# A recurrence of 1024 steps: a filler matmul or a denser piece of attention in each step

## The chip, the cores and the metric

The kernel runs on one core of a Trainium2 chip. The metric is device time in microseconds of one execution. Three runs of the kernel before took 1089.88, 1085.83 and 1089.57 us; the median is 1089.57.

## The reference, cut to what matters

The model is a small image network: four blocks, each a token mixer and a feed-forward part, on x of shape (2, 32, 32, 32): two images, 1024 pixels each, 32 channels. The third block's feed-forward part (L2 in the kernel) is a recurrence over the 1024 pixels in order. From inputs W, V, gamma, beta it computes, in words:

```
x : (2, 1024, 32)            # after a layer norm
wx = batch_norm(x @ W.T)     # gamma, beta; statistics over all tokens
h_0 = 0
h_t = sigmoid(wx_t + h_(t-1) @ V.T)      # t = 1 .. 1024, for both images
x = x + h
```

The fourth block's mixer (L3) is attention in windows of 8x8 and 16x16 pixels and across windows. Its input is the residual stream with the states of that recurrence added:

```
sim = einsum('bnhid,bnhjd->bnhij', qh * SCALE, kh) + pos
attn = softmax(sim, axis=-1)
out = einsum('bnhij,bnhjd->bnhid', attn, vh)
```

Since a window covers pixels next to each other, its attention can start as soon as the recurrence has passed its last pixel.

## The kernel before, in words

The program is a sequence of blocks. `recurrent(tag, swept, use, beside)` is called for L0 (swept, with another algorithm: many segments advanced at once, three sweeps, lines 896 to 926) and for L2 (not swept: one step after another). This case is about the second call.

Its first block does the layer norm (`Norm.pe`, with 11 filler matmuls from `keep_streaming`, line 95, which multiply a constant tile of ones into a dead PSUM bank), the product with W (line 786), batch statistics and the scaled input, written into `yx`. Column pair t of `yx` holds, in its upper 32 rows, the input of step t for both images and, in its lower 32 rows, the state.

Its second block is the loop. Step t is one matmul of TensorE, `v` (64x32, V and the identity stacked) times two columns of `yx`, into PSUM (line 844), and one sigmoid of ScalarE from PSUM back into the next two columns (line 856). The matmul waits for the semaphore `state`, the sigmoid for `preact`. In fp32 a matmul is two weight loads and two matmul records in the trace.

`Front` holds the part of the L3 attention that is done within the loop. `front.pe` and `front.pe_bulk` are Python generators that issue TensorE's instructions for it piece by piece: each `yield` ends a piece. From step HALF + 5 = 517 on, the loop calls `next(others)` once after each step, so that at most one piece stands between two steps; `for _ in range(n): yield` is n steps without a piece, in which VectorE does the work that the next piece waits for. The first half's pixels are taken at step 512, three eighths more at 896 (`BULK`), the last 128 after the loop. The pieces are: products of the query and key weights (line 1676), transposes of x (1509) and of the normed x (1519), projections (1592), values and across-window products (1694, 1700, 1705), scores (1447, 1449), transposes of the scores (1610). TensorE's queue is in program order, so a piece stands ahead of the next step's matmul.

VectorE's side (`dve`, `dve_bulk`) is the layer norm of a part, copies out of PSUM, the biased scores (1457) and their shift by the least (1470), each behind semaphores. `rest` is the block after the loop, with the remaining attention.

Of the kernel before, what the change touches and what calls it, by code (L numbers as in the profile page):

```python
# [15 lines left out]
NB, SIDE, C = 2, 32, 32  # L16
# [722 lines left out]
def more(nc, io, loc):  # L739
    ctx, sig, sb, ps, chain, unchain, Norm = (loc[k] for k in ("ctx", "sig", "sb", "ps", "chain", "unchain", "Norm"))  # L740
    keep_streaming = loc["keep_streaming"]
# [6 lines left out]
    def recurrent(tag, swept, use, beside):  # L748
# [5 lines left out]
        with ExitStack() as st:  # L754
# [8 lines left out]
            with ExitStack() as s2:  # L763
# [6 lines left out]
                with nc.Block() as block:  # L770
# [8 lines left out]
                    def _(pe):  # L779
# [51 lines left out]
            with ExitStack() as s2:  # L831
                p_z = ps(tag + "p_z", [128, 2, BANK], stack=s2)
                if not swept:

                    HALF, BULK = T // 2, T - 128
                    front = beside(s2, by_batch)
                    with nc.Block() as block:
                        @block.tensor
                        def _(pe):
                            others = front.pe(pe)  # L840
                            for t in range(T):
                                if t:
                                    pe.wait_ge(s("state"), t)
                                pe.matmul(p_z[0:C, t % 2, 0:NB], v[:, 0:C], yx[:, NB * t:NB * (t + 1)], start=True, stop=True).then_inc(s("preact"), 1)  # L844
                                if t == BULK + 5:
                                    others = itertools.chain(others, front.pe_bulk(pe))
                                if t > HALF + 4:
                                    next(others, None)
                            for _ in others:
                                pass  # L850

                        @block.scalar
                        def _(act):
                            for t in range(T):
                                act.wait_ge(s("preact"), t + 1)
                                act.activation(yx[0:C, NB * (t + 1):NB * (t + 2)], p_z[0:C, t % 2, 0:NB], ACT.Sigmoid).then_inc(s("state"), 1)  # L856
# [495 lines left out]
    with ExitStack() as st:  # L1352
# [97 lines left out]

        def biased(dve, banks, u):
# [20 lines left out]
        def shifts_until(u):  # L1472
            return u + 1 - sum(1 for a in BY_ACT if a <= u)

        class Front:
# [28 lines left out]
            def turn(self, pe, part):  # L1504

                a, b = self.PARTS[part]
                pe.wait_ge(sig["part_added"], 3 * part + 3)
                for t in range(a, b):
                    ins = pe.transpose(self.p_tok[:, t * R:(t + 1) * R], x[:, t * 128:(t + 1) * 128], ident[0:R, 0:R])
                    if t == b - 1:  # L1510
                        ins.then_inc(sig["part_turned"], 1)
                    yield

            def turn_back(self, pe, part):

                a, b = self.PARTS[part]
                pe.wait_ge(sig["part_scaled"], part + 1)
                for t in range(a, b):
                    ins = pe.transpose(self.p_back[:, t % 4 * 128:(t % 4 + 1) * 128], xn_two[:, t - a], ident[:])
# [69 lines left out]
            def project(self, pe, part, g, dst):  # L1589
                a, b = self.PARTS[part]  # L1590
                for r, n, src in strips(g, xo[:, WITHIN[g]], 4 * a, 4 * (b - a)):
                    last = pe.matmul(dst[:, r * SIDE:(r + n) * SIDE], aqk[:, WITHIN[g]], src, start=True, stop=True)
                last.then_inc(sig["qk_made"], 1)
# [8 lines left out]
            def turn_scores(self, pe, u):  # L1602

                pe.wait_ge(sig["at_shifted"], u + 1)
                for n in range(2):
                    s = 2 * u + n
                    if s >= 2:
                        pe.wait_ge(sig["weights_in"], s - 1)
                    for j in range(NJ):
                        last = pe.transpose(self.turn_banks[n][:, j * 128:(j + 1) * 128], scored[:, u, j, n * 128:(n + 1) * 128], ident[:])  # L1610
                        if j == NJ - 1:
                            last.then_inc(sig["scores_turned"], 1)
                        yield
# [6 lines left out]
            def score_early(self, pe, u):  # L1620
                for n in range(1 if units[u][0] == 2 else 2):
                    for j in range(NJ):
                        ins = score(pe, self.early_banks[j], u, j, n)
                        if units[u][0] == 2 or n == 1:
                            ins.then_inc(sig["at_scores"], 1)
                    yield

            def value_pieces(self, pe, part, p_v):

                for slot, g, tiles in ((0, 2, (4 + part, 6 + part)), (1, 0, (4 + 2 * part, 5 + 2 * part))):  # L1630
                    for n, t in enumerate(tiles):
                        last = pe.matmul(p_v[:, (2 * slot + n) * JC:(2 * slot + n + 1) * JC], value_tokens(g, t), av[:, slot], start=True, stop=True)
                        if (slot, n) == (1, 1):
                            last.then_inc(sig["e_made"], 1)
                        yield

            def across_pieces(self, pe, part, p_3, p_1):

                cols = 3 * HEADS * HC
                for n in range(4):  # L1640
                    for b in range(NB):
                        last = pe.matmul(p_1[b * 64:(b + 1) * 64, n * cols:(n + 1) * cols], window1(8 + 4 * part + n), ae1[:, b], start=True, stop=True)
                    yield
                cols = NB * 3 * HEADS * HC
                for n in range(2):
                    last = pe.matmul(p_3[:, n * cols:(n + 1) * cols], window3(part, 2 + n), ae3[:], start=True, stop=True)
                    if n == 1:
                        last.then_inc(sig["e_made"], 1)
                    yield
# [21 lines left out]
            def pe(self, pe):  # L1671

                p_q, p_e = self.p_q, self.p_e
                pe.wait_ge(sig["load_at"], 16 * 14)
                for k in range(2):
                    last = pe.matmul(p_q[:, 0, k * 128:(k + 1) * 128], aq[:, k], ak[:, k], start=True, stop=True)
                    if k == 1:
                        last.then_inc(sig["qk_made"], 1)
                    yield
                yield from self.turn(pe, 0)  # L1680
                for _ in range(24):
                    yield
                yield from self.turn_back(pe, 0)
                for _ in range(6):
                    yield
                pe.wait_ge(sig["qk_read"], 1)
                for k, g in enumerate((2, 0)):
                    pe.wait_ge(sig["xo_made"], k + 1)
                    self.project(pe, 0, g, p_q[:, k])
# [713 lines left out]
```

## Time and profile before

| | |
|---|---|
| median of three runs | 1089.57 us |
| the profiled execution | 1091.56 us |
| its span, first to last instruction | 1089.6 us |
| TensorE busy | 726.1 us, 67% |
| ScalarE, VectorE, GpSimd busy | 447.6, 436.1, 255.3 us |
| mean granted clock of TensorE | 0.676 |
| matmuls of line 844 | 269.2 us busy, 2048 records |

The profile is of one execution. In it, PE is TensorE's matmuls and PEld its weight loads (they overlap), DVE is VectorE, ACT ScalarE, POOL GpSimd. PEclk is the share of TensorE's full clock (2.4 GHz) that was granted; it has two levels, 1.0 and 0.5, and a value between them is a mean over a stretch with both. Idle time of an engine stands with what ended it, behind an arrow.

### The profile page before, as it was taken

To read this page: it belongs to the slowest core of one execution; us is meant where nothing else is said; L and a number is where in the kernel's file an instruction comes from. 1 tells how busy PE (TensorE), PEld (TensorE's weight loads), DVE (VectorE), ACT (ScalarE), POOL (GpSimd) and SP (SyncE) were. 2 spreads that over 40 slices of the span, in tenths; PEclk is the share of its full clock that TensorE was granted. 3 is DMA by queue.
4 is the path that set the end of the run, shared out by engine and by line. 5 is a ranking of instruction groups with operands and counts; after the bars stand their busy time and mean duration, and the time that the engine had idled before them with its cause. 6 is when DMAs were issued, how large, how long until landed. Compare 5 with 4: busy or idle time off the path is not lost. (4 is left out here: it accounts for less than half of the span.)

```text
span 1089.6 us, 11684 instructions
## 1 busy us (share of the span) xinstructions
PE 726.1 (67%) x4350; PEld 414.4 (38%) x4361; DVE 436.1 (40%) x733; ACT 447.6 (41%) x1480; POOL 255.3 (23%) x153
## 2 busy tenths in 40 slices
PE   7907878888886787555555555558786555675776
PEld 4302333333343444233333333336554333453443
DVE  4697999999856554400000000021242000210653
ACT  4446767676635542333333333332222333223541
POOL 3378988898900000200000000000000000000310
PEclk9957999999995595655555555555555555555796
DMA  3020000000000000200000000000000000000000
GB/s 68 2 58 0 1 0 1 0 1 0 1 3 3 1 22 10 74 1 1 1 0 1 1 1 1 1 0 1 1 1 1 1 0 1 1 1 1 2 23 10
DMA packets 10017, 7.92 MB, mean 7 GB/s; under 512 B 7378, under 2 KB 8514, under 8 KB 9672
## 3 DMA queue, kind: packets, MB, share of 16 engines
q1 hardware_dynamic: 9960, 7.18, 2.7%
q8 instruction: 34, 0.56, 0.2%
q14 instruction: 23, 0.19, 0.1%
HBM read 5.34 MB, written 0.26 MB: 5 GB/s over the span
## 5 line engine op out<-in xcount | busy, mean ns | idle before, releaser
L844 PE MATMUL L2p_z<-L2yx,L2v 64*32 64x2 f32 x2048 | 269.2, 199 | 231.1 <-ACT L2yx L856 226.1
L856 ACT ACTIVATE L2yx<-L2p_z 32x2 f32<-32x2 f32 x1024 | 165.0, 161 | 383.5 <-PE L2p_z L844 383.5
L844 PEld LDWEIGHTS L2p_z<-L2yx,L2v 64*32 64x32 f32 x2048 | 181.4, 136 | 334.2 <-ACT L2yx L856 317.2
L630 POOL TENSOR_TENSOR hc<-hs,cb 128x1024 f32<-128x1024 f32 x64 | 149.4, 2355 | 20.9 <-DVE hs L613 20.9
L1499 DVE COPY xn<-L2yx 32x512 f32<-32x512 f32 (+1 forms) x2 | 0.8, 384 | 366.4 <-ACT L2yx L856 366.4
L1499 POOL COPY xn<-L2yx 32x128 f32<-32x128 f32 x1 | 0.3, 283 | 544.4 <-SPq L1827 544.4
L557 PE MATMUL p_y<-hc,ident 128*128 128x512 f32 x256 | 122.4, 600 | 5.0 <-DVE y_seq L596 2.8
L613 DVE TENSOR_TENSOR_SCAN hs<-d_a,p_bb 128x1024 f32<-128x1024 f32 x48 | 109.8, 2287 | 7.2 <-ACT d_a L580 1.1
L584 ACT ACTIVATE cb<-p_cb 128x1024 f32<-128x1024 f32 x64 | 65.0, 1016 | 6.0 <-PE p_cb L547 5.7
L557 PEld LDWEIGHTS p_y<-hc,ident 128*128 128x128 f32 x256 | 47.7, 191 | 49.9 <-issue 31.3
L580 ACT ACTIVATE d_a<-step,decay 128x1016 f32<-128x1016 f32 x48 | 54.6, 1138 | 24.1 <-DVE hs L613 23.5
L602 DVE TENSOR_TENSOR p_bb<-drive,p_bb 128x1024 f32<-128x1024 f32 x48 | 58.0, 1208 | 6.3 <-PE p_bb L541 6.3
L547 PE MATMUL p_cb<-c_parts,pick 96*128 96x512 bf16 x128 | 39.6, 391 | 11.9 <-ACT d_bu L589 10.5
L541 PE MATMUL p_bb<-b_parts,pick 96*128 96x512 bf16 x96 | 29.6, 391 | 20.4 <-DVE hs L613 19.4
L625 POOL TENSOR_TENSOR d_bu<-drive,d_bu 128x1024 f32<-128x1024 f32 x16 | 37.9, 2369 | 5.1 <-ACT d_bu L589 5.1
L906 PE MATMUL L0p_z<-L0yx,L0v 64*32 64x64 f32 x192 | 30.3, 305 | 9.9 <-PEq L770 4.4
L613 DVE TENSOR_TENSOR_SCAN hs<-p_bb,d_bu 128x1024 f32<-128x1024 f32 x16 | 36.2, 2264 | 0.0
L541 PEld LDWEIGHTS p_bb<-b_parts,pick 96*128 96x128 bf16 x96 | 8.3, 99 | 46.5 <-DVE hs L613 31.0
L906 PEld LDWEIGHTS L0p_z<-L0yx,L0v 64*32 64x32 f32 x192 | 17.5, 140 | 22.3 <-ACT L0yx L926 16.2
L926 ACT ACTIVATE L0yx<-L0p_z 32x64 f32<-32x64 f32 x96 | 20.1, 214 | 13.3 <-PE L0p_z L906 12.9
L547 PEld LDWEIGHTS p_cb<-c_parts,pick 96*128 96x128 bf16 x128 | 11.1, 98 | 37.9 <-ACT d_bu L589 18.8
L589 ACT ACTIVATE d_bu<-p_cb 128x1024 f32<-128x1024 f32 x16 | 16.4, 1024 | 18.1 <-PE p_cb L564 18.1
(485 smaller groups left out, 916.0 us busy)
## 6 DMA issues: line engine op xcount, KB each, us to landing
y_seq<-in_pick SPq DMA_DIRECT2D x1, 768.0 KB
b_parts<-part SPq DMA_DIRECT2D x3, 256.0 KB, 3.7
c_parts<-part SPq DMA_DIRECT2D x3, 256.0 KB, 4.4
pos<-in_pos SPq DMA_DIRECT2D x1, 512.0 KB, 3.6
ao<-in_at_o SPq DMA_DIRECT2D x1, 512.0 KB, 4.1
L1w<-in_L_w SPq DMA_DIRECT2D x1, 297.0 KB
L3w<-in_L_w SPq DMA_DIRECT2D x1, 297.0 KB
x_tok<-in_x SPq DMA_DIRECT2D x2, 128.0 KB, 3.0
```

What stands on the lines that cost most here:

```text
L541: last = pe.matmul(p_bb[:, u % 2, h * BANK:(h + 1) * BANK], pick[:, n], b_parts[:, k, c], start=True, stop=True)
L547: last = pe.matmul(p_cb[:, h * BANK:(h + 1) * BANK], pick[:, n], c_parts[:, k, c], start=True, stop=True)
L557: last = pe.matmul(p_y[:, c], ident[:], hc[:, v % RING, c], start=(n == 0), stop=(n == NS - 1))
L580: act.activation(dst[:, :, 1:L], src[:, :, 1:L], ACT.Exp, scale=decay[:, k, n:n + 1]).then_inc(sig["d_a"], 1)
L584: act.activation(cb[:, u % RING], p_cb[:], ACT.Copy).then_inc(sig["p_cb_read"], 1)
L602: dve.tensor_tensor(p_bb[:, u % 2], drive[:, k, c0:c0 + UC], p_bb[:, u % 2], ALU.mult).then_inc(sig["d_bu"], 1)
L613: dve.tensor_tensor_scan(hs[:, u % RING], decays, inputs, 0.0, ALU.mult, ALU.add).then_inc(sig["scanned"], 1)
L625: pool.tensor_tensor(d_bu_of(u), drive[:, k, c0:c0 + UC], d_bu_of(u), ALU.mult).then_inc(sig["d_bu_pool"], 1)
L630: pool.tensor_tensor(hc[:, u % RING], hs[:, u % RING], cb[:, u % RING], ALU.mult).then_inc(sig["hc"], 1)
L844: pe.matmul(p_z[0:C, t % 2, 0:NB], v[:, 0:C], yx[:, NB * t:NB * (t + 1)], start=True, stop=True).then_inc(s("preact"), 1)
L856: act.activation(yx[0:C, NB * (t + 1):NB * (t + 2)], p_z[0:C, t % 2, 0:NB], ACT.Sigmoid).then_inc(s("state"), 1)
L906: pe.matmul(p_z[0:C, f, 0:NB * n], v[:, 0:C], by_batch[:, cols], start=True, stop=True).then_inc(s("preact"), 1)
```

## The change

Each step of the L2 loop now carries either one filler, a bf16 matmul of 128x128 weights and 512 columns into a dead bank (`fill(FILL)`), or one piece of attention. Which of them is decided when the program is built: `beats` is a list of (nanoseconds, columns) of the steps so far, with 473 ns and 520 columns assumed for a filler step; each `yield` of a generator now says ahead of a piece how many nanoseconds and columns its step is to have (0, 0 for a rest); and `goes` lets the piece in only if the columns of the latest steps that fill 3413 ns, the piece's own among them, come to 3290 or more. Else the step takes a filler and the piece waits for the next.

The pieces themselves are made larger or smaller to fit: two or three transposes instead of one, four matmuls of the across-window products instead of one or two, projections cut into matmuls of 128 columns, the 256 keys of a score into two halves (`score_half`). The rests are recounted. Waits on semaphores move behind the yield. Step 0 is followed by five fillers. Ahead of the loop, 11 fillers follow the product with W, and 4 more the semaphore `shift`, which VectorE raises before it writes the scaled input. Both halves of the step's PSUM output now lie in bank 0 (`p_step`), since the filler writes bank 1. The L0 recurrence is not changed.

```diff
@@ recurrent, first block
                         if swept:
                             beside.pe_sum(pe, p_a)
                             beside.pe_square_sum(pe, p_a)
+                        else:
+                            keep_streaming(pe, p_a[:, 0:BANK], 11)
+                            pe.wait_ge(*at("shift", 1))
+                            keep_streaming(pe, p_a[:, 0:BANK], 4)
@@ recurrent, the loop
+                    FILL, STEP, WINDOW, LEAST = 512, 473, 3413, 3290
+                    p_step = p_z[0:C, 0].rearrange("p (n b) -> p n b", b=NB)
...
+                            def fill(columns):
+                                parts = (columns + BANK - 1) // BANK
+                                each = columns // parts // 16 * 16
+                                for _ in range(parts):
+                                    pe.matmul(p_z[:, 1, 0:each], stream[:, 0:128], stream[:, 0:each], start=True, stop=True)
+
+                            beats = [(STEP, FILL + 8)] * 8
+
+                            def goes(ns, columns):
+                                room, work = WINDOW - ns, columns + 8
+                                for length, did in reversed(beats):
+                                    part = min(length, room)
+                                    work += did * part / length
+                                    room -= part
+                                    if room <= 0:
+                                        break
+                                return work >= LEAST
+
                             others = front.pe(pe)
+                            ns, columns = next(others)
                             for t in range(T):
                                 if t:
                                     pe.wait_ge(s("state"), t)
-                                pe.matmul(p_z[0:C, t % 2, 0:NB], v[:, 0:C], yx[:, NB * t:NB * (t + 1)], start=True, stop=True).then_inc(s("preact"), 1)
+                                pe.matmul(p_step[:, t % 2], v[:, 0:C], yx[:, NB * t:NB * (t + 1)], start=True, stop=True).then_inc(s("preact"), 1)
+                                if t == 0:
+                                    fill(5 * BANK)
+                                    continue
                                 if t == BULK + 5:
+                                    assert not columns
                                     others = itertools.chain(others, front.pe_bulk(pe))
-                                if t > HALF + 4:
-                                    next(others, None)
-                            for _ in others:
-                                pass
+                                    ns, columns = next(others, (0, 0))
+                                if t > HALF + 4 and columns and goes(ns, columns):
+                                    beats.append((ns, columns + 8))
+                                    ns, columns = next(others, (0, 0))
+                                    continue
+                                if t > HALF + 4 and not columns:
+                                    ns, columns = next(others, (0, 0))
+                                beats.append((STEP, FILL + 8))
+                                if t < T - 1:
+                                    fill(FILL)
@@ Front.turn_scores, as an example of a generator
-                pe.wait_ge(sig["at_shifted"], u + 1)
                 for n in range(2):
                     s = 2 * u + n
-                    if s >= 2:
-                        pe.wait_ge(sig["weights_in"], s - 1)
                     for j in range(NJ):
+                        if j % 2 == 0:
+                            yield 600, 4 * 128
+                        if (n, j) == (0, 0):
+                            pe.wait_ge(sig["at_shifted"], u + 1)
+                        if j == 0 and s >= 2:
+                            pe.wait_ge(sig["weights_in"], s - 1)
                         last = pe.transpose(self.turn_banks[n][:, j * 128:(j + 1) * 128], scored[:, u, j, n * 128:(n + 1) * 128], ident[:])
                         if j == NJ - 1:
                             last.then_inc(sig["scores_turned"], 1)
-                        yield
@@ Front.pe, one of the recounted rests
                 yield from self.turn(pe, 0)
-                for _ in range(24):
-                    yield
+                yield from rests(28)
                 yield from self.turn_back(pe, 0)
```

What stands in TensorE's queue where the loop begins: `L2p_z<-L2yx,L2v` is the step, `stream` the filler, `L2p_w` the product with W. Before:

```order
L127 MATMUL L2p_b<-ident,xn_tok 64x128 x8
L786 MATMUL L2p_w<-xn,L2w 32x512 x4
L770 UNCONDITIONAL_BRANCH
L838 UNCONDITIONAL_BRANCH
L844 MATMUL L2p_z<-L2yx,L2v 32x2 x518
```

And after the change:

```order
L127 MATMUL L2p_b<-ident,xn_tok 64x128 x8
L786 MATMUL L2p_w<-xn,L2w 32x512 x4
L95 MATMUL L2p_a<-stream 128x512 x15
L770 UNCONDITIONAL_BRANCH
L844 UNCONDITIONAL_BRANCH
L869 MATMUL L2p_z<-L2yx,L2v 32x2
L850 MATMUL L2p_z<-stream 128x512 x5
L869 MATMUL L2p_z<-L2yx,L2v 32x2
L850 MATMUL L2p_z<-stream 128x512
```

Where 518 steps stood next to each other, each is now followed by a filler, and 15 fillers stand ahead of the loop (11 before the wait for `shift` and 4 behind it).

In TensorE's queue where a unit's scores are transposed (`scored` into the banks `atp_tok` and `atp_back`; `q` and `xo` are the scores' operands). Before:

```order
L1447 MATMUL atp_q<-xo,q 128x256 x2
L1447 MATMUL atp_e<-xo,q 128x256 x2
L844 MATMUL L2p_z<-L2yx,L2v 32x2 x3
L1610 MATMUL atp_tok<-ident,scored 128x128
L844 MATMUL L2p_z<-L2yx,L2v 32x2
L1610 MATMUL atp_tok<-ident,scored 128x128
L844 MATMUL L2p_z<-L2yx,L2v 32x2
L1610 MATMUL atp_tok<-ident,scored 128x128
```

And after the change:

```order
L869 MATMUL L2p_z<-L2yx,L2v 32x2
L1673 MATMUL atp_tok<-ident,scored 128x128 x2
L869 MATMUL L2p_z<-L2yx,L2v 32x2
L1673 MATMUL atp_tok<-ident,scored 128x128 x2
L869 MATMUL L2p_z<-L2yx,L2v 32x2
L1673 MATMUL atp_back<-ident,scored 128x128 x2
L869 MATMUL L2p_z<-L2yx,L2v 32x2
L850 MATMUL L2p_z<-stream 128x512
L869 MATMUL L2p_z<-L2yx,L2v 32x2
L850 MATMUL L2p_z<-stream 128x512
```

The transposes go in pairs, three pairs in a row and then fillers; a unit's eight transposes take four steps with a piece instead of eight. In the whole loop 945 steps carry a filler, 78 a piece, and the last neither.

## Rows read from the trace of the kernel before

**Rows 1.** The page, the span in 40 slices: busy shares and clock in tenths.
```profile
PE   7907878888886787555555555558786555675776
...
PEclk9957999999995595655555555555555555555796
```

**Rows 2.** The page's costliest groups: count, busy us, mean ns, idle before and releaser.
```profile
L844 PE MATMUL L2p_z<-L2yx,L2v 64*32 64x2 f32 x2048 | 269.2, 199 | 231.1 <-ACT L2yx L856 226.1
L856 ACT ACTIVATE L2yx<-L2p_z 32x2 f32<-32x2 f32 x1024 | 165.0, 161 | 383.5 <-PE L2p_z L844 383.5
```

**Rows 3.** Timeline, the loop's first two steps and last: start us, length us, engine.
```profile
454.58 0.23 PE L844 MATMUL L2p_z<-L2yx,L2v 64*32 64x2 f32 x2 [5.00 <-PEq L770]
...
456.05 0.26 PE L844 MATMUL L2p_z<-L2yx,L2v 64*32 64x2 f32 x2 [1.24 <-ACT L2yx L856]
...
1004.15 0.16 ACT L856 ACTIVATE L2yx<-L2p_z 32x2 f32<-32x2 f32 x1 [0.35 <-PE L2p_z L844]
```

**Rows 4.** A window: length; busy us of PE, PEld, DVE, ACT, POOL; granted clock; DMA.
```profile
750.00:775.00 25.00, 21.90 (x146) 18.46 (x146) 1.33 (x6) 6.65 (x42) 0.00 (x0) 0.50 0.00 1
```

**Rows 5.** Timeline, one step of the loop, and the 24th after it.
```profile
470.42 0.18 PEld L844 LDWEIGHTS L2p_z<-L2yx,L2v 64*32 64x32 f32 x2 [0.34 <-ACT L2yx L856]
470.42 0.26 PE L844 MATMUL L2p_z<-L2yx,L2v 64*32 64x2 f32 x2 [0.25 <-ACT L2yx L856]
470.72 0.16 ACT L856 ACTIVATE L2yx<-L2p_z 32x2 f32<-32x2 f32 x1 [0.35 <-PE L2p_z L844]
...
482.74 0.18 PEld L844 LDWEIGHTS L2p_z<-L2yx,L2v 64*32 64x32 f32 x2 [0.34 <-ACT L2yx L856]
```

**Rows 6.** Timeline, two matmul pairs of one shape, at full and at half clock.
```profile
330.65 0.27 PE L997 MATMUL L0p_a<-sm,ones 64*64 64x1 f32 x2
...
332.06 0.37 PE L1001 MATMUL L0p_a<-sm,ones 64*64 64x1 f32 x2 [1.13 <-DVE sm L1009]
```

**Rows 7.** Timeline, fillers of line 95: ten at full clock, five at half.
```profile
1057.21 2.32 PE L95 MATMUL L3p_b<-stream 128*128 128x512 bf16 x10 [0.16 <-issue]
...
426.11 2.34 PE L95 MATMUL e2p_b<-stream 128*128 128x512 bf16 x5 [0.33 <-issue]
```

**Rows 8.** Timeline, steps with a piece: a 128x128 product; a 16-column one.
```profile
721.84 0.18 PEld L844 LDWEIGHTS L2p_z<-L2yx,L2v 64*32 64x32 f32 x2 [0.23 <-issue]
...
722.76 0.18 PEld L844 LDWEIGHTS L2p_z<-L2yx,L2v 64*32 64x32 f32 x2 [0.23 <-issue]
...
752.35 0.61 PE L1694 MATMUL atp_e<-av,xo 128*128 128x16 f32 x2
...
752.88 0.18 PEld L844 LDWEIGHTS L2p_z<-L2yx,L2v 64*32 64x32 f32 x2
```

**Rows 9.** Timeline of the last matmuls ahead of the loop, and windows there.
```profile
448.51 1.06 PE L786 MATMUL L2p_w<-xn,L2w 32*32 32x512 f32 x8 [0.76 <-ACT xn L173]
...
450.00:452.00 2.00, 0.00 (x0) 0.00 (x0) 1.54 (x5) 0.29 (x1) 0.00 (x0) 0.85 1.06 369
```

**Rows 10.** Timeline of VectorE, its first work after the norm of the first part.
```profile
739.64 1.35 DVE L1549 COPY xo<-atp_back 128x512 f32<-128x512 f32 x3 [10.01 <-PE atp_back L1519]
```

**Rows 11.** Timeline behind the loop, TensorE's first product.
```profile
1004.62 1.19 PE L1566 MATMUL atp_tok<-L2yx,centre 32*128 32x128 f32 x4 [0.51 <-PEq L837]
```

**Rows 12.** Windows, columns as in rows 4.
```profile
350.00:355.00 5.00, 4.31 (x29) 2.53 (x28) 4.58 (x24) 2.90 (x15) 0.00 (x0) 0.50 0.00 0
440.00:442.00 2.00, 2.00 (x8) 0.84 (x7) 1.97 (x2) 0.00 (x0) 0.00 (x0) 0.71 0.00 0
1060.00:1065.00 5.00, 3.07 (x17) 1.27 (x18) 0.42 (x1) 1.95 (x4) 0.00 (x0) 1.00 0.32 103
1070.00:1075.00 5.00, 3.57 (x30) 2.81 (x31) 1.89 (x8) 0.00 (x0) 0.00 (x0) 0.76 0.00 0
```

**Rows 13.** One of three groups of four transposes before 1028, and a window there.
```profile
1026.92 1.06 PE L1869 MATMUL L2p_z<-ident,araw 128*128 128x128 f32 x4
...
1028.00:1029.00 1.00, 1.00 (x19) 0.79 (x20) 0.97 (x2) 0.22 (x1) 0.00 (x0) 0.87 0.00 0
```

More of the change, by code:

```diff
@@ L855, in _ @@
                                 act.wait_ge(s("preact"), t + 1)
[L856 removed]
+                                act.activation(yx[0:C, NB * (t + 1):NB * (t + 2)], p_step[:, t % 2], ACT.Sigmoid).then_inc(s("state"), 1)
                         @block.vector
@@ L1449, in score, with score_half @@
             return pe.matmul(dst[:, n * 128:(n + 1) * 128], q[rows, 1, own], xo[rows, 1, own], start=True, stop=True)
+        def score_half(pe, dst, u, j, n):
+            t = units[u][1]
+            rows = slice(32 * j, 32 * j + 32)
+            k0 = t // 2 * KEYS + n * 128
+            return pe.matmul(dst[:, n * 128:(n + 1) * 128], q[rows, 0, t * 128:(t + 1) * 128], xo[rows, 0, k0:k0 + 128], start=True, stop=True)
         def biased(dve, banks, u):
@@ L1473, in shifts_until, with rests @@
             return u + 1 - sum(1 for a in BY_ACT if a <= u)
+        def rests(n):
+            for _ in range(n):
+                yield 0, 0
         class Front:
@@ L1692, in pe @@
-                for slot, g in enumerate((2, 0)):
-                    for t in range(4):
-                        pe.matmul(p_e[:, slot, EC + t * JC:EC + (t + 1) * JC], value_tokens(g, t), av[:, slot], start=True, stop=True)
-                        yield
-                cols = NB * 3 * HEADS * HC
-                for f in range(2):
-                    for w in range(2):
-                        n = f * 2 + w
-                        pe.matmul(p_e[:, 0, n * cols:(n + 1) * cols], window3(f, w), ae3[:], start=True, stop=True)
-                        yield
+                    yield from self.project(pe, 0, g, p_q[:, k], k + 1)
@@ new lines, in pe @@
+                    yield from rests(3)
+                cols = NB * 3 * HEADS * HC
+                for t in range(4):
+                    if t % 2 == 0:
+                        yield 680, 2 * 4 * (JC + cols)
+                    n = t % 2 * 2 + t // 2
+                    pe.matmul(p_e[:, 0, EC + t * JC:EC + (t + 1) * JC], value_tokens(2, t), av[:, 0], start=True, stop=True)
+                    pe.matmul(p_e[:, 0, n * cols:(n + 1) * cols], value_tokens(2, t), ae3[:], start=True, stop=True)
@@ L1702, in pe @@
+                yield 600, 4 * 4 * JC
+                for t in range(4):
+                    pe.matmul(p_e[:, 1, EC + t * JC:EC + (t + 1) * JC], value_tokens(0, t), av[:, 1], start=True, stop=True)
                 cols = 3 * HEADS * HC
                 for w in range(8):
+                    if w % 2 == 0:
+                        yield 600, 2 * 4 * cols
                     for b in range(NB):
                         last = pe.matmul(p_e[b * 64:(b + 1) * 64, 1, w * cols:(w + 1) * cols], window1(w), ae1[:, b], start=True, stop=True)
-                        if (w, b) == (7, 1):
-                            last.then_inc(sig["e_made"], 1)
@@ L1719, in pe @@
                     if u:
                         yield from self.turn_scores(pe, u - 1)
-                        for _ in range(3):
-                            yield
+                        yield from rests(5)
                 yield from self.turn_scores(pe, FIRST - 1)
```

114 lines of the change are left out of this document (58 added, 56 removed).

## The prediction

> **What bounds the kernel now.** I read the page's 40 slices first. From slice 17 to slice 36 TensorE's row reads 5 or a little more where attention is worked in, and the granted clock reads 5 (the lower level, 1.2 GHz) [rows 1]. The costliest groups say what runs there: line 844, a matmul of two columns, and line 856, its sigmoid, 1024 times each, each waiting mostly for the other [rows 2]. This is a recurrence, so no other engine can shorten it; its first matmul starts at 454.58 and its last sigmoid at 1004.15, ending at 1004.31: 549.7 us, half the span [rows 3]. The windows by stretch show the clock at 0.50 in all of it, even at 750 to 775 where TensorE is busy 21.90 of 25 us [rows 4].
>
> The timeline gives one step: loads and matmuls start at 470.42, the sigmoid at 470.72. The 24 steps from 470.42 to 482.74 take 12.32 us, 513 ns each: about 300 ns on TensorE up to the sigmoid's start, 160 of sigmoid, the other 50 until the next load begins [rows 5]. 1024 such steps are 525.6 us; the remaining 24 us are the first step, 1.5 us long because ScalarE loads its table in it [rows 3], and the pieces of attention, which at this clock lengthen the step that carries them.
>
> **The step at the other clock.** The change adds no shortcut to the chain. What it can alter is the clock at which the 300 ns on TensorE run. The nearest rows are a pair of small matmuls with 64x64 weights and one moving column, one at the full clock, one at half: 0.27 us against 0.37 [rows 6]. The recurrence's weights have half as many columns (64x32), so I take half the difference, 50 ns. A bare step would be 513 - 50 = 463 ns. Ends: 0 saved (if the 300 ns were latency that no clock touches) gives 513; 100 saved, the whole of the pair's difference, gives 413.
>
> **The filler in the step.** Each step without a piece now issues one 128x512 bf16 matmul behind its own (945 times). At the full clock ten of them take 2.32 us, 232 ns each; at half, 0.43 [rows 7]. The step's own pair is done at 0.26 - 0.05 = 0.21 us, and 0.21 + 0.232 = 0.44, under the 0.463 at which the next state arrives. So it hides behind the sigmoid, by 20 ns. Rows of the piece steps say how much room a late one has: the step's next load began at 752.88 while the piece's matmuls ran until 752.96 [rows 8]. I take 470 ns, 7 for the squeeze; ends 455 and 500 (a filler whose own weight load of 100 ns is not hidden, less what the pair's overlap gives back). If the cover were gone at half clock, the piece's work starts 0.19 us into the step, its weight load 0.13 and stream 0.43 follow, less 0.08 of overlap: 0.67, I take 650 ns, 137 more than today.
>
> **The pieces.** The 125 steps that carry a piece in before become 78 with denser ones: two transposes, four half scores, projections cut to 128 columns. In before, a step with a 128x128 fp32 product, as many columns as most of the new pieces, takes 0.92 us [rows 8]. At twice the clock the part over the bare step at least halves in its array work: 0.92 becomes 0.46 to 0.92. The planner's own figures for the 78 pieces sum to 46.0 us, 589 ns each, inside these ends; I take them. Both ends kept: 0.47 to 0.75 each, -9 to +13 us.
>
> **What surrounds it.** Fifteen fillers are put before the recurrence: eleven after line 786 and four after the shift. In before the last matmul there ends at 449.57 and TensorE is idle until the loop's first, at 454.58, while VectorE and ScalarE scale the input [rows 3, 9]. 15 x 0.232 = 3.5 us of fillers lie in those 5.0 us and cost nothing; without that cover they would cost 3.5. The five fillers after step 0 (1.2 us) lie in the 1.5 us of the first step. Their part is the state of the clock: in before it was 1.00 to 450 and fell in 450 to 452, after TensorE stood still [rows 9]. It now enters the recurrence without such a stop.
>
> VectorE's work between pieces has to fit into fewer nanoseconds per counted step. After the layer norm of the first part VectorE sits 10.01 us until the turned-back tokens come [rows 10]. The 24 rests of 513 ns there (12.3 us) become 28 of 470 (13.2), so there is no new wait; the other rests are lengthened in the same manner, by a tenth or more where they were short. A stop of TensorE there would matter, since everything behind it, the step's matmul too, is in its queue; I find none. At the far end, the stretch behind the last step starts at half clock in before: 1.19 us at 1004.62, on the way to VectorE's last norm [rows 11]. Full clock there saves up to half of it, 0.6; where the clock then falls and rises moves, worth up to 3 either way. I take -1.
>
> **The sum**, against the profiled execution (span 1089.6, 1091.56 in all): first step 1.5; 945 x 0.470 = 444.2; 78 x 0.589 = 46.0; together 491.7 against 549.7, so -58; with the tail -59. That makes a span of 1030.6 and an execution of 1032.5. The median of the runs shown is 1089.57, 2.0 under the profiled one, so I predict 1030.5.
>
> **Will the clock stay up?** The sum stands on this. TensorE's busy share alone does not tell the clock in this trace. In the earlier recurrence (350 to 355) TensorE is busy 4.31 of 5 us with 64-column matmuls and the clock stays 0.50; in 1070 to 1075 it falls (0.76) with 3.57 of 5 busy, with small matmuls. It stays 1.00 in 1060 to 1065 with only 3.07 busy, which were 128- and 512-column matmuls; and it rises in 440 to 442, under fillers back to back [rows 12]. So long matmuls go with the full clock, and short ones, however busy the engine, with half. With the filler every step has a long one, over 213 of its 470 ns (512 columns at 2.4 GHz); no row shows such a mixture held for 500 us, which is where the doubt lies. Started at half clock the mixture would resemble the earlier recurrence (busy most of the time, 0.50 for 30 us) more than the back-to-back fillers under which the clock rose. So a fall would probably not be mended within the recurrence.
>
> A page's rule bears on this. The Trainium skill, "TensorE: Matmul & The Clock Gate" (Part 4, PE-mode transpose), says that transposes do not count as busy for the clock the way matmuls do. By that rule the stretch of 24 two-transpose steps is where the clock would fall; that is the second rival. The trace only half agrees: the clock rose at 1028, in a stretch (1022.9 to 1028.6) in which 12 of the matmuls were transposes of 128 columns and the others scores and values [rows 13]. By the rule the time would be near the second rival's; by the rows the sum stands.
>
> **Rivals.**
> Cold all along: the clock falls before the first steps and the filler is no longer hidden. 1.5 + 945 x 0.65 + 78 x 0.85 (between the filler step's 0.65 and the 0.92 of rows 8) = 682, +132: 1222. For it: nothing holds the clock there today. Against: 15 fillers and no stop over 1 us. Chance 0.06.
> It falls among the pieces and stays down (the slower case below): each full-clock step has won 43 ns, each step at half loses 137, so it decides at step n with 43n = 137(1024 - n), about 780. A fall at step 620, in the small-matmul pieces: 599 fillers at 0.47, 20 pieces at 0.59, then 346 at 0.65 and 58 at 0.85, with the first step 569, +19: about 1109. Those pieces stream 192 to 256 columns in a step, half a filler. Against: the planner puts six fillers between them. Chance of a fall before 780: 0.08, slower. After it (the second part starts at step 901: 844 x 0.47 + 57 x 0.59 + 101 x 0.65 + 21 x 0.85 + 1.5 = 515): -34, about 1055, chance 0.05.
> The filler is not hidden: 0.50 a step, 472.5 + 46 + 1.5 = 520, -30: 1060. For it: only 20 ns of room by the rows. Chance 0.06.
> The clock holds but the step does not shorten (latency, not clock): 0.513 a step, 532, -18: 1072. Against: the pair of rows 6. Chance 0.03.
>
> **Chances and range.** The forecast has 0.72; its own range, from 460 to 485 ns a step and the ends of the pieces and tail, is 1019 to 1048. To leave out no more than two in ten I reach over the late fall and the unhidden filler: 1019 to 1062. About 0.5% (5 us) is what a measurement of this kernel can tell from no change. Faster: 0.72 + 0.06 + 0.05 + 0.03, less a little: 0.84; slower 0.14; same 0.02.
>
> **What would show it.** Right: windows of 25 us between 475 and 1000 with a granted clock of 1.00, step loads 470 ns apart, sigmoid 0.25 us after the load's start, a filler of 0.23 us ending before the next load. Wrong: a stretch at 0.50 with steps of 0.65 us (then where it begins names the piece at fault), or the wait of a step's load put down to TensorE itself rather than to the sigmoid of line 892, or a bare step still at 513 ns at full clock.

## The result, and the profile after

The changed kernel took 1146.78 us (median of four runs, 1145.59 to 1152.9), the kernel before 1087.7 (four runs beside it). The ratio is 1.0554, interval 1.0508 to 1.06: slower by 5.5%, where 1030.5 us was predicted. The profiled execution took 1146.74 us with a span of 1145.0.

The page's slices of the changed kernel, the answer to [rows 1]; 28.6 us each:

```profile
PE   7828888878868778999999999999999999999786
...
PEclk9958999999985788999999999855555555555777
```

The recurrence is in slices 17 to 37. The clock row has two parts there: 9 up to slice 25, then 5 from slice 27 to 37. TensorE's busy row reads 9 in both. The costliest groups, the answer to [rows 2] (busy us, mean ns, idle before and releaser):

```profile
L850 PE MATMUL L2p_z<-stream 128*128 128x512 bf16 x886 | 418.5, 473 | 0.0
L892 ACT ACTIVATE L2yx<-L2p_z 32x2 f32<-32x2 f32 x1024 | 165.3, 161 | 441.8 <-PE L2p_z L869 441.8
...
L869 PE MATMUL L2p_z<-L2yx,L2v 64*32 64x2 f32 x2048 | 244.4, 187 | 22.9 <-ACT L2yx L892 22.0
```

Of the fillers' 949 matmuls (five of them at step 0) 886 records are in the trace, so busy times of TensorE are a little low here. The sigmoid itself is as it was (161 ns), and its wait for TensorE grew from 383.5 to 441.8 us: 58 us of the 59 that were lost. By stretches, with columns as in [rows 4] (busy us of PE, PEld, DVE, ACT, POOL; granted clock; DMA):

```profile
450.00:452.00 2.00, 1.09 (x5) 0.31 (x4) 1.84 (x6) 1.34 (x2) 0.00 (x0) 1.00 0.81 288
500.00:525.00 25.00, 24.24 (x158) 12.17 (x159) 0.00 (x0) 8.56 (x53) 0.00 (x0) 1.00 0.01 2
...
733.00:736.00 3.00, 3.00 (x23) 2.02 (x22) 0.00 (x0) 0.81 (x5) 0.00 (x0) 0.99 0.00 0
736.00:740.00 4.00, 3.53 (x18) 2.55 (x19) 0.00 (x0) 0.65 (x4) 0.00 (x0) 0.50 0.00 0
900.00:925.00 25.00, 24.06 (x101) 9.67 (x102) 0.00 (x0) 5.49 (x34) 0.00 (x0) 0.50 0.00 1
```

The clock enters the recurrence at 1.00, where [rows 9] had 0.85 in the same two microseconds, and stays there for 283 us. At 736 it falls to the lower level (1.2 GHz) and does not come back before 1067, behind the loop. ScalarE's count in 25 us, one for each step, goes from 53 to 34.

One step at either clock, beside [rows 5]. First the full clock:

```profile
500.33 0.22 PE L869 MATMUL L2p_z<-L2yx,L2v 64*32 64x2 f32 x2
...
500.48 0.39 PE L850 MATMUL L2p_z<-stream 128*128 128x512 bf16 x1
500.59 0.16 ACT L892 ACTIVATE L2yx<-L2p_z 32x2 f32<-32x2 f32 x1 [0.31 <-PE L2p_z L869]
500.80 0.14 PEld L869 LDWEIGHTS L2p_z<-L2yx,L2v 64*32 64x32 f32 x2 [0.23 <-ACT L2yx L892]
```

Then half:

```profile
900.17 0.18 PEld L869 LDWEIGHTS L2p_z<-L2yx,L2v 64*32 64x32 f32 x2 [0.43 <-ACT L2yx L892]
...
900.37 0.61 PE L850 MATMUL L2p_z<-stream 128*128 128x512 bf16 x1
900.47 0.16 ACT L892 ACTIVATE L2yx<-L2p_z 32x2 f32<-32x2 f32 x1 [0.57 <-PE L2p_z L869]
900.90 0.18 PEld L869 LDWEIGHTS L2p_z<-L2yx,L2v 64*32 64x32 f32 x2 [0.43 <-ACT L2yx L892]
```

At the full clock the next step's load starts 0.47 us after this one's, 0.05 after the sigmoid's end at 500.75: the filler hides. At half the sigmoid ends at 900.63 and the load starts at 900.90, when the filler is nearly done (900.98): the filler, not the sigmoid, now sets the step, 0.73 us. (The profile still puts the wait down to ScalarE, whose semaphore came long before.) The first 592 steps took 282.0 us, from first sigmoid to the 593rd, where the kernel before took 311.5; the remaining 431 took 324.9, before 236.8. That is -29.5 and +88.1.

What TensorE did ahead of the fall (steps 587 to 590, timeline of PE):

```profile
731.82 0.22 PE L869 MATMUL L2p_z<-L2yx,L2v 64*32 64x2 f32 x2
731.97 0.39 PE L1762 MATMUL atp_e<-av,xo 128*128 128x16 f32 x2
732.22 0.40 PE L1763 MATMUL atp_e<-ae,xo 128*128 128x48 f32 x2
732.46 0.36 PE L1762 MATMUL atp_e<-av,xo 128*128 128x16 f32 x2
732.66 0.40 PE L1763 MATMUL atp_e<-ae,xo 128*128 128x48 f32 x2
733.00 0.22 PE L869 MATMUL L2p_z<-L2yx,L2v 64*32 64x2 f32 x2
733.15 0.39 PE L850 MATMUL L2p_z<-stream 128*128 128x512 bf16 x1
733.47 0.22 PE L869 MATMUL L2p_z<-L2yx,L2v 64*32 64x2 f32 x2
```

These are the value pieces: four products, two of 16 columns and two of 48, each with its own 128 columns of weights. The next matmul starts 0.25 and 0.20 us after a product of 16 columns begins and 0.24 us after one of 48, so the columns do not set the pace. In this step the weight loads are busy 1.11 of 1.20 us (731.8 to 733.0), so they probably do. The step takes 1.18 us (731.82 to 733.00), where `yield 680, 2 * 4 * (JC + cols)` gives it 680 ns. A filler step follows, then the next such piece (733.47 to 734.64), and 1.3 us after it the clock is down.

### The profile page after: what moved, and what is told of

It reads as the page before. It is cut to its first block and busy times, and to the rows that moved or that the text cites. A ratio compares the mean times of both kernels' runs of the same rounds, so it can differ in the third digit from the quotient of the medians.

```text
span 1145.0 us, 13643 instructions
## 1 busy us (share of the span) xinstructions
PE 991.0 (87%) x5299; PEld 478.7 (42%) x5373; DVE 436.4 (38%) x733; ACT 447.9 (39%) x1480; POOL 255.6 (22%) x153
## 5 line engine op out<-in xcount | busy, mean ns | idle before, releaser
L850 PE MATMUL L2p_z<-stream 128*128 128x512 bf16 x886 | 418.5, 473 | 0.0
L892 ACT ACTIVATE L2yx<-L2p_z 32x2 f32<-32x2 f32 x1024 | 165.3, 161 | 441.8 <-PE L2p_z L869 441.8
L869 PEld LDWEIGHTS L2p_z<-L2yx,L2v 64*32 64x32 f32 x2048 | 156.6, 118 | 308.9 <-ACT L2yx L892 300.7
L869 PE MATMUL L2p_z<-L2yx,L2v 64*32 64x2 f32 x2048 | 244.4, 187 | 22.9 <-ACT L2yx L892 22.0
L850 PEld LDWEIGHTS L2p_z<-stream 128*128 128x128 bf16 x949 | 94.5, 100 | 15.2
L95 PE MATMUL p_d<-stream 128*128 128x512 bf16 x19 | 6.9, 546 | 25.5 <-DVE step L471 25.5
```

The source lines that it names most:

```text
L850: pe.matmul(p_z[:, 1, 0:each], stream[:, 0:128], stream[:, 0:each], start=True, stop=True)
L869: pe.matmul(p_step[:, t % 2], v[:, 0:C], yx[:, NB * t:NB * (t + 1)], start=True, stop=True).then_inc(s("preact"), 1)
L892: act.activation(yx[0:C, NB * (t + 1):NB * (t + 2)], p_step[:, t % 2], ACT.Sigmoid).then_inc(s("state"), 1)
```

## The experiments

The theory: the clock is held by long streams of columns (fillers, 128-column products and transposes), not by TensorE being busy. The value pieces are priced at little more than half their real time, so the count of columns by stretch lets them in, two of them with one filler between, and for a while TensorE does mostly weight loads. Where an expectation has a letter, A is this theory, and A2 its nearest variant, that a step much longer than a usual one drops the clock whatever is in it. Other rivals: the transposes, which the prediction weighed as the place of a fall; and the change as a whole being worthless, with or without a fall. The experiments are numbered in the order in which they were set up, e1 to e10. "Before" ran beside them at 1091.0 (e1 to e4), 1090.35 (e5 to e8) and 1087.82 (e9, e10).

**Value pieces one by one (e1).** Those of the first part only, each matmul a piece of its own at the price of a step:

```diff
-                    if t % 2 == 0:
-                        yield 680, 2 * 4 * (JC + cols)
                     n = t % 2 * 2 + t // 2
+                    yield 473, 4 * JC
                     pe.matmul(p_e[:, 0, EC + t * JC:EC + (t + 1) * JC], value_tokens(2, t), av[:, 0], start=True, stop=True)
+                    yield 473, 4 * cols
                     pe.matmul(p_e[:, 0, n * cols:(n + 1) * cols], value_tokens(2, t), ae3[:], start=True, stop=True)
-                yield 600, 4 * 4 * JC
                 for t in range(4):
+                    yield 473, 4 * JC
```

> The three value pieces of the first part (steps 587, 589, 596), each four or eight fp32 matmul pairs in one step, are cut into twelve pieces of one matmul, 473 ns and 64 or 192 columns each, so that the planner puts six or seven fillers between them. Theory A (the clock fell because these pieces last 1.17 us where the plan says 0.68 and 0.60, so that too few columns came in that stretch): the clock stays at 1.00 past step 596; if it also passes the second part's value pieces, the loop takes about 492 us and the whole 1030 to 1036; if it falls there (step 942), 82 steps at 735 ns cost 21 more, 1050 to 1060. Theory B (the mixture of fillers and pieces is too thin as such, and the value pieces only happened to come first): the clock falls at some other piece before step 760 and stays down, 1110 to 1150.

Measured: 1052.22 us (1052.89, 1027.48, 1052.35, 1052.08). One of its runs lies apart from the other three, so no ratio is given. In the profiled one the clock passed the old place and fell at 908, behind the two value pieces of the second part (line 1703), which were left as they were:

```profile
902.12 0.62 PE L1703 MATMUL atp_e<-av,xo 128*128 128x16 f32 x4
902.67 0.22 PE L869 MATMUL L2p_z<-L2yx,L2v 64*32 64x2 f32 x2
```

and a window:

```profile
908.00:909.00 1.00, 1.00 (x7) 0.51 (x6) 0.00 (x0) 0.25 (x3) 0.00 (x0) 0.71 0.00 0
```

From 909 on it was 0.50. Those two steps (901.97 to 902.67 is one) took 0.70 us at a price of 500 ns. The fall follows the value pieces to where they are next underpriced, here with seven fillers between the two. 1050 to 1060 us had been expected for a fall there. The time of 1027.48 is that of the next kernel, which has no fall, so that run probably had none either; only the profiled one has a trace.

**Both parts one by one (e2).** The same, and in `value_pieces`:

```diff
-                    yield 500, 2 * 4 * JC
                     for n, t in enumerate(tiles):
+                        yield 473, 4 * JC
```

> As the one before, and the second part's two value pieces (steps 942, 950) cut into four of one matmul too. Theory A: clock 1.00 from before the loop to its end, 1030 to 1036. Theory B: as before, 1110 to 1150.

Measured: 1031.68 us (1027.48 to 1034.7), ratio 0.9477, interval 0.9428 to 0.9526. Repeated on another chip (e10):

> The kernel with single value pieces in both parts again, on the same chip as the one with a filler in every step, to compare the two. Theory A: clock 1.00 throughout, 1027 to 1035, 10 to 20 us under the other.

Measured: 1029.55 us (six runs, 1026.64 to 1034.7), ratio 0.9456, interval 0.9426 to 0.9487. The slices of the first, and a window late in its recurrence:

```profile
PEclk9966999999999559799999999999999999999788
```

```profile
900.00:925.00 25.00, 24.25 (x176) 13.45 (x178) 0.91 (x4) 8.38 (x52) 0.00 (x0) 1.00 0.01 1
```

The clock is 1.00 to the loop's end. This stretch and that of the changed kernel have about the same busy share, 24.25 and 24.06 of 25 us (records are missing in both), and different clocks. From the first step's matmul (452.80) to the last sigmoid's end (942.46) it is 489.7 us, 60.0 less than before; the sum had said 491.7. All pieces but those of the values are the changed kernel's, so the transposes in pairs, three pairs in a row, are run at the full clock: they do not drop it here.

**No filler in the steps (e3).** `if t < T - 1: fill(FILL)` is left out; fillers ahead of the loop and denser pieces stay.

> The filler of each step is left out; the pieces, their places and the twenty fillers before and at step 0 stay. Both theories: without the long matmul the clock falls within a few steps of the loop's start, steps are 513 ns, the 78 pieces take about 0.9 us each at half clock: 946 x 0.513 + 78 x 0.9 + 1.5 = 557 against 550 before, so 1090 to 1100. It prices what the filler costs at half clock: the changed kernel's steps after its fall took 735 ns. If it stays at full clock instead, 1025 to 1035, the filler is not needed at all.

Measured: 1093.13 us, ratio 1.0034 (1.0009 to 1.006), that is, at most 0.6% from before.

```profile
500.00:525.00 25.00, 12.72 (x99) 8.58 (x98) 0.00 (x0) 7.91 (x49) 0.00 (x0) 0.50 0.00 1
```

The clock fell at 454.78, in the loop's first steps, and 49 steps went into 25 us, 0.51 each as before. The 15 fillers ahead of the loop and the denser pieces alone bring nothing; without the fillers in the steps there is neither the gain nor the loss.

**A filler of 256 columns (e4).** `fill(FILL // 2)`.

> The filler has 256 columns instead of 512, everything else as in the changed kernel. If a step with TensorE nearly always busy were enough, the clock would hold at first and the time be under 1147. If the length of the streams counts, the clock falls near the loop's start, and since 256 columns at half clock (213 ns) fit beside the sigmoid, steps are 513 to 540 ns: 1090 to 1120.

Measured: 1106.44 us, ratio 1.0155 (1.0111 to 1.0199).

```profile
455.00:459.00 4.00, 3.69 (x28) 2.01 (x27) 0.00 (x0) 1.29 (x8) 2.76 (x2) 1.00 0.01 2
500.00:525.00 25.00, 25.00 (x147) 13.51 (x146) 0.00 (x0) 7.74 (x48) 0.00 (x0) 0.50 0.00 1
```

Eight steps at the full clock in these 4 us, then the fall at 459.1, after 13 steps, and half clock to the loop's end with TensorE busy 25.00 of 25 us by the profile. Half the stream does not hold the clock, and a busy row of 100% does not bring it back. Ahead of the fall TensorE was busy 3.69 of 4 us, less than with the whole filler (25.00 of 25 at 1.00 in e7, whose filler records are all in the trace), so this run alone does not tell the shorter stream from the bit of idle time beside it. A step at half clock is 0.52 us, so this filler is nearly hidden there.

**Fillers inside the value pieces (e5).** This separates A from A2: the value pieces stay whole, and get longer still by fillers among their matmuls (`self.dense(pe)` is one 128x512 matmul of `stream`).

```diff
                     pe.matmul(p_e[:, 0, n * cols:(n + 1) * cols], value_tokens(2, t), ae3[:], start=True, stop=True)
+                    self.dense(pe)
                 yield 600, 4 * 4 * JC
                 for t in range(4):
                     pe.matmul(p_e[:, 1, EC + t * JC:EC + (t + 1) * JC], value_tokens(0, t), av[:, 1], start=True, stop=True)
+                    if t % 2:
+                        self.dense(pe)
```

and one before the second matmul of `value_pieces`.

> The value pieces of both parts stay whole, in the steps where the changed kernel has them, but fillers are put among their matmuls (two in each of the first three, one in each of the two later ones), so that the steps become longer still (about 1.2 us to 1.65) and have long streams in them. Theory A (few columns in that stretch, because the pieces last longer than planned): the clock holds at 1.00, and the time is that of the kernel with single values or a little less, 1028 to 1036. A rival, A2 (it is the length of a step without the loop's own filler, or the two pieces' nearness to each other, not what they stream): the clock falls there as before, 1140 to 1155.

Measured: 1036.02 us (1031.57 to 1039.16), ratio 0.951, interval 0.9471 to 0.955. One of the value steps in the timeline of PE:

```profile
732.55 0.22 PE L870 MATMUL L2p_z<-L2yx,L2v 64*32 64x2 f32 x2
...
732.94 0.40 PE L1769 MATMUL atp_e<-ae,xo 128*128 128x48 f32 x2
733.18 0.38 PE L864 MATMUL L2p_z<-stream 128*128 128x512 bf16 x1
...
734.08 0.22 PE L870 MATMUL L2p_z<-L2yx,L2v 64*32 64x2 f32 x2
```

and the window behind it:

```profile
735.00:740.00 5.00, 5.00 (x37) 3.23 (x37) 0.00 (x0) 1.13 (x7) 0.00 (x0) 1.00 0.00 0
```

This step took 1.53 us, 30% longer than those ahead of the fall, and the clock stayed 1.00 here and to the loop's end. A2 falls; A stands. With long streams put into the same steps, the times of all four runs are those of a kernel without a fall: the long streams are what was missing.

**Ten fillers in one step of the half-clock stretch (e6).** `fill(10 * BANK if t == 760 else FILL)`, in the changed kernel.

> The changed kernel with ten fillers instead of one at step 760, behind the first part's pieces. If half clock is kept only because the mixture of one filler and one step does not lift it, a burst lifts it: it costs about 4 us, and the steps from 760 to the second part's value pieces (942) take 472 instead of 735 ns, 48 less; with a second fall there 1098 to 1108, without it 1075 to 1085. If the clock comes back by something else, or the mixture falls again at once, 1145 to 1155.

Measured: 1096.92 us; its four runs spread from 1080.59 to 1110.64, so no ratio is given. Windows of the fastest, which is the profiled one, ahead of the burst, around it and behind:

```profile
840.00:860.00 20.00, 20.00 (x87) 8.52 (x86) 2.08 (x4) 4.35 (x27) 0.00 (x0) 0.50 0.00 1
...
863.00:867.00 4.00, 4.00 (x12) 1.52 (x12) 0.00 (x0) 0.16 (x1) 0.00 (x0) 0.51 0.00 0
...
870.00:890.00 20.00, 20.00 (x127) 9.66 (x126) 0.00 (x0) 6.89 (x43) 0.00 (x0) 1.00 0.00 1
...
940.00:965.00 25.00, 25.00 (x181) 14.32 (x180) 2.55 (x8) 8.08 (x51) 0.00 (x0) 1.00 0.00 1
```

A hundred microseconds and more of filler steps had not lifted the clock; one stop of the recurrence for ten fillers back to back (863.35, 4.06 us) did, and the same filler steps then held it. So the filler is enough to keep the clock and not enough to win it back. A likely reason, not tested by itself: at half clock the step takes 0.73 us with the same one filler, so it streams less in the same time. The prediction had this right.

The last window holds the two value pieces of line 1703, whole and at the same steps as in e1 (953.45 and 957.45, 0.70 us each). In e1 the clock fell behind them; here it stayed 1.00 to 996.6, past the loop's end. The same underpriced pieces can thus go either way, and what decides it was not found. Of the other three runs two, 1105.15 and 1110.64, are near the 1098 to 1108 expected for a second fall; the third, 1088.69, fits neither case. None of the three was traced.

**Fillers in the kernel before (e7).** Its own pieces, with a filler in each step without a piece, and the same 15 and 5 ahead:

```diff
-                                if t > HALF + 4:
-                                    next(others, None)
+                                rest = next(others, True) if t > HALF + 4 else True
+                                if rest and t < T - 1:
+                                    keep_streaming(pe, p_z[:, 1], 5 if t == 0 else 1)
```

> The kernel before, with its own pieces (one matmul or one group each, up to 28 steps in a row), plus the twenty fillers around the loop's start and a filler in each step that has no piece. Theory A: its first 517 steps run at 472 ns, and the clock falls in the run of value and across pieces (step 569 on) or already at 519; the rest takes 735 ns a step without a piece: 1120 to 1145. It tells what the filler alone is worth without denser, spaced pieces. If it holds, 1030 to 1040.

Measured: 1151.48 us, ratio 1.0584 (1.0529 to 1.0638).

```profile
475.00:500.00 25.00, 25.00 (x160) 12.18 (x159) 0.00 (x0) 8.54 (x53) 0.00 (x0) 1.00 0.00 1
...
702.00:703.00 1.00, 1.00 (x7) 0.51 (x6) 0.91 (x3) 0.33 (x3) 0.00 (x0) 0.75 0.00 0
```

The fall came at 702.5, after the first six pieces in a row (698.1 to 701.1: two 128-column products, four single transposes of 64 columns). The clock came back at 733.2, behind 2 us of 256-column projections (line 1598), and fell again at 740.1 among the single value matmuls. Six pieces side by side, as small as these, were enough to lose it. The time is 6 us above the range that was expected.

**The good version without the count (e8).** e2 with `LEAST = 0`: every piece goes in as soon as it is there.

> The kernel with single value pieces, but the planner's condition is always true: a piece goes in as soon as it is there, twelve value pieces and four across pieces in a row from step 573. Theory A: the clock falls there, 1135 to 1155, though no step is longer than planned; if it holds, the spacing is not needed, 1025 to 1035.

Measured: 1154.28 us, ratio 1.0576 (1.0523 to 1.0628).

```profile
700.00:702.00 2.00, 2.00 (x13) 0.97 (x12) 1.73 (x9) 0.52 (x4) 0.00 (x0) 0.80 0.00 0
```

I had placed the fall at step 573; it came at 701.2, behind the first four pieces: two products and two pairs of 64-column transposes, next to each other (697.17 to 699.1). In e2 the count puts fillers behind the products and between the transposes, and the clock holds. So the spacing is as necessary as the pieces' size. The two products alone, side by side, did not drop the clock in e2; the 64-column transposes behind them did the rest, and whether by their few columns or because they are transposes no run tells.

**A filler in every step, pieces or not (e9).** e7 with the filler unconditional, no spacing:

> The kernel before with its own pieces, the twenty fillers around the loop's start, and a filler in every step, also behind a piece; no planner. Theory A: every step has a 512-column stream, and the longest run of thin steps (a 16- or 24-column product in each) lasts about 0.15 + 0.26 + 0.23 = 0.64 us with one filler in it, which is thinner in time than the 472 ns step but not as thin as two 1.17 us pieces: I expect the clock to hold, at 899 steps of 472 ns and 125 of about 0.60 to 0.70, 505 to 513 for the loop against 550, so 1040 to 1052. If 28 thin steps in a row are too thin, the clock falls there, 1140 to 1170.

Measured: 1192.85 us (1186.2 to 1197.23), ratio 1.0946 (1.091 to 1.0982). A miss: I expected the clock to hold. It did, past the place of e7's fall, up to the first value matmuls:

```profile
726.34 0.22 PE L849 MATMUL L2p_z<-L2yx,L2v 64*32 64x2 f32 x2
726.49 0.40 PE L1700 MATMUL atp_e<-av,xo 128*128 128x16 f32 x2
726.74 0.38 PE L95 MATMUL L2p_z<-stream 128*128 128x512 bf16 x1
727.04 0.22 PE L849 MATMUL L2p_z<-L2yx,L2v 64*32 64x2 f32 x2
```

The windows:

```profile
725.00:729.00 4.00, 4.00 (x29) 2.42 (x29) 0.00 (x0) 1.13 (x7) 0.00 (x0) 1.00 0.02 4
...
730.00:735.00 5.00, 5.00 (x24) 3.06 (x23) 0.00 (x0) 0.64 (x4) 0.00 (x0) 0.50 0.00 0
```

A step with one 16-column product and a filler takes 0.70 us instead of 0.47, so the same filler is a smaller part of it; after four of these the clock fell. The time is above even the 1140 to 1170 given for a fall. One filler to a step is thus no guarantee. It fits the idea that the share of the time with streams counts, which is the changed kernel's own, but that share was not measured as such, and fillers alone do not order the runs: e5's value step has two in 1.53 us, this one has one in 0.70, slightly more, and only this one lost the clock. Here such steps stand in a row, there a filler step lies between two of them, and e5's products also stream more columns; which of these matters was not separated.

## Why the prediction was wrong

Wrong in sign and by 116 us, by one step of it: "Will the clock stay up?".

**The step that failed.** The answer to that question stood on the 78 pieces at "the planner's own figures", 589 ns each, and on their placing. Those figures were an input of the count that was to hold the clock, and I checked them only for their sum. For most pieces they hold or are too high (a 128-column product or projection is priced 570 ns and takes 0.57 us, a pair of 128-column transposes 600 and takes 0.52). For the value pieces they do not: 1.18 us against 680 ns at the full clock, and 0.70 against 500 in the second part. A small error for the sum, some 2 us; for the clock it was the whole matter, since a piece that takes nearly twice its price nearly halves the columns per time in its step. e1, e2 and e5 show it: with the value pieces cut up, or with fillers inside them, the clock held where it had fallen. [rows 8] had the price: a pair of 16-column records from 752.35 to the next load at 752.88 is 0.53 us at half clock. Even halved, four of them are 1.06 us; with the 0.15 ahead of them, 1.21. I used these rows for the room of a late piece and not for this.

**A misread place.** Against the rival of a fall I wrote that the planner puts six fillers between small-matmul pieces. It does so for the across-window ones, from step 603 on. The two value pieces at steps 587 and 589 have one filler between them, and eight projections stand 5 to 15 steps ahead.

**The rival that came true** was named, with its fall at step 620, 1109 us and a chance of 0.08 before step 780. The fall came at step 592. The time was 38 us above the rival's, mostly from one term: the filler step at half clock, 0.65 by my sum, took 0.735. Behind the fall are 62 pieces and 369 other steps; 369 x 0.085 = 31 us. The filler begins 0.20 us into the step as I had it, but takes 0.61, where I had put 0.13 and 0.43, 0.56 together, and a step of 0.67 that I then rounded down to 0.65. The 62 pieces took (324.9 - 369 x 0.735) / 62 = 0.87 us each, by my value 0.85. With 0.472 and 0.735 a step wins 41 ns at the full clock and loses 222 at half, so the step from which a fall no longer decides is 864 instead of 780.

**What was right.** Step at the full clock: 470 ns predicted, 472 measured, with the filler hidden. The pieces at the full clock: with 1.5 us for the first step the loop was to take 491.7 us, and where the clock held (e2) it took 489.7. VectorE: in e2, from 480 to 940, all of the 15.1 us in which a step's matmul waited idle are put to the sigmoid, none to VectorE. Fillers ahead of the loop at no cost: in the changed kernel the loop's first matmul starts at 452.58, 2.0 us earlier than in [rows 3], and the clock enters at 1.00. Tail: from the last sigmoid's end to the end of the span 84.1 us after, 85.3 before, -1.2 where I took -1. That agreement is partly luck: the same kernel's tail is 83.2 us in e2 and 87.5 in e10. That a fall would not mend itself: shown by e6. Busy share doesn't tell the clock: TensorE is busy 25.00 of 25 us at 0.50 in e4 and at 1.00 in e7.

**The rule on transposes.** The Trainium skill, "TensorE: Matmul & The Clock Gate" (Part 4, PE-mode transpose), says that transposes do not count as busy for the clock as matmuls do. These runs do not bear it out for fp32 transposes of 128 columns: e2 ran all of them, in pairs three steps in a row (1.55 us without a filler, from 799.30), at 1.00. Longer rows of them were not run, and e8, where the clock fell behind two products and two pairs of 64-column transposes, does not speak against the rule. The same page of the Trainium skill ("Why this matters for your kernels") looks for a fall behind idle gaps of TensorE. Here it fell with no gap: TensorE is busy 3.00 of 3.00 us right before.

**What stays open.** How much stream a stretch needs was not measured, and no run gave the whole value pieces their true price. e1's run of 1027.48 us, e6's spread, and the pieces of line 1703 that drop the clock in e1's trace and not in e6's show that near the edge the same code goes either way. Whether the 15 fillers ahead of the loop are needed was not tested: e3 shows only that without fillers in the steps they bring nothing, and no run has the fillers in the steps without them. Since the steps' fillers did not lift the clock in e6, a loop that is entered at half clock might stay there.

## What to carry to other kernels

Where a latency-bound loop is to be kept at the full clock by fillers, price each piece that displaces a filler from a timeline row of its own kind: an fp32 product with 128 columns of weights and few moving ones (16 or 48 here) costs 0.20 to 0.25 us at the full clock. Pieces that are mostly weight loads should be single and apart, or carry fillers inside. Reckon what a fall costs before adding fillers: here 41 ns won a step against 222 lost, and the clock came back within the loop only under long matmuls back to back (e6, e7).

## What the runs showed of the hardware

- TensorE's busy share does not tell its clock: 25.00 of 25 us at 0.50 (e4), 25.00 of 25 at 1.00 (e7).
- The mixture of a two-column pair and one 512-column matmul keeps the clock at 1.00 for 490 us, well-spaced pieces among it (e2), and stays at 0.50 for 130 us once it has fallen (e6). There ten 512-column matmuls back to back lifted it.
- With no filler the clock fell at 454.78, with 256 columns a step at 459.1, with 512 and underpriced pieces at 735.96, with 512 and single, spaced value pieces not before the loop's end. The loop begins at about 452 in each.
- An fp32 product of 128x128 weights takes the same time for 16 columns as for 48, 0.20 to 0.25 us one behind the other at the full clock.
